# Cross-attention unit: both outer key products together, the sixth projection with the next unit's first, the middle key product behind them

## The reference, cut to what matters

```
q_hk  = (hidden_q @ Wq.T).reshape(B, S, H, K)
q_big = rope(einsum('bshk,hkq->bshq', q_hk, w_kc_q))      # 192 wide per head
q_r   = einsum('bshq,hqr->bhsr', q_big, W_qr)
k_r   = einsum('bld,hdr->bhlr', rope(kv_c), W_kr)
attn  = softmax(einsum('bhsr,bhlr->bhsl', q_r, k_r))
ctx_c = einsum('bhsl,bld->bhsd', attn, rope(kv_c))
out   = (einsum('bhsd,hkd->bhsk', ctx_c, w_kc_kv) -> B, S, H*K) @ Wo.T
```

## Time and profile before

| what | value |
|---|---|
| median of 3 runs | 451.5 us (450.04 to 451.88) |
| profiled execution, its own time | 454.02 us |
| span of that execution in the trace | 452.2 us |
| mean granted TensorE clock | 0.943 of full speed |
| attention units in the span | 211.3 to about 367.6 us |
| busy over the span | PE 82%, DVE 74%, ACT 47%, POOL 31% |

### The profile page before, as it was taken

One profiled execution on the slowest core, in us unless ns is written; L12 is line 12 of the kernel. 1 busy time (PEld: TensorE's weight loads), 2 busy tenths in 40 slices (PEclk: granted clock), 3 DMA queues, 4 the chain that ended last, 5 costly groups with the idle time before them and its releaser, 6 DMA issues.

```text
span 452.2 us, 10550 instructions
## 1 busy us (share of the span) xinstructions
PE 373.0 (82%) x3676; PEld 257.6 (57%) x3677; DVE 335.7 (74%) x836; ACT 213.0 (47%) x467; POOL 139.3 (31%) x149
## 2 busy tenths in 40 slices
PE   2497888833777778997999999999999989729995
PEld 1376666731344445774466475575664778516784
DVE  6849999888889889579776886887777525672453
ACT  1689999461577788684021131132122221324441
POOL 1110000023477774311092440431421410143334
PEclk9999999855699999999999999999999999957999
DMA  8995680402146551271022022021120201333011
GB/s 259 404 407 196 235 321 5 188 1 64 37 157 223 181 161 48 77 250 40 0 94 94 1 95 92 4 94 43 53 94 10 87 1 48 140 95 92 25 37 37
DMA packets 17183, 50.77 MB, mean 112 GB/s; under 512 B 2104, under 2 KB 6464, under 8 KB 15088
## 3 DMA queue, kind: packets, MB, share of 16 engines
q1 hardware_dynamic: 14272, 42.46, 26.3%
q0 software_dynamic: 2864, 7.68, 5.9%
HBM read 43.44 MB, written 6.69 MB: 111 GB/s over the span
## 4 chain that ended last, share of the span: by engine, by line
PE 56%; ACT 11%; DVE 10%; issue 8%; DMA 7%; POOL 5%; SPq 2%; DVEq 0%; ACTq 0%; POOLq 0%
PE bank L960 16%; PE bank L1174 8%; PE bank L976 6%; PE bank L1048 5%; DMA raw<-in_L_ffn_w_dram 3%; ACT W L1207 3%; PE bank L987 3%; PE bank L1001 2%; POOL y_rows L591 2%; PE bank L819 2%; PE bank L1027 2%; PE bank L1011 2%; ACT pnat L1193 2%; PE bank L830 1%; POOL xg L584 1%
## 5 line engine op out<-in xcount | busy, mean ns | idle before, releaser
L1714 DVE TENSOR_TENSOR roped<-bank,cst 128x512 f32<-128x512 f32 x96 | 61.1, 684 | 29.0 <-PE bank L960 28.0
L612 POOL TENSOR_TENSOR WE<-WE,wT 128x512 f32<-128x512 f32 x32 | 42.6, 1359 | 81.6 <-DMA WE<-_L_ffn_expert_masks_dram 81.6
L960 PE MATMUL bank<-XNT_hi,AW_hi 128*128 128x512 f32 x96 | 41.8, 435 | 0.5 <-DVE XNT_lo L1766 0.5
L1343 ACT ACTIVATE qrT<-bank 128x512 f32<-128x512 f32 x16 | 8.7, 596 | 62.2 <-PE bank L987 62.2
L960 PE MATMUL bank<-XNT_lo,AW_hi 128*128 128x512 f32 x96 | 37.8, 393 | 0.0
L960 PE MATMUL bank<-XNT_hi,AW_lo 128*128 128x512 f32 x96 | 37.5, 391 | 0.0
L976 PE MATMUL bank<-roped,MW 128*64 128x512 f32 x128 | 31.0, 605 | 0.0
L1337 ACT ACTIVATE prob<-prob 128x512 f32<-128x512 f32 x16 | 10.1, 632 | 44.3 <-DVE prob L1724 44.3
L1048 PE MATMUL bank<-VW,ctxT 128*128 128x256 f32 x128 | 30.7, 385 | 0.0
L584 POOL DMA_INDIRECT xg<-x_rows,owner_b x23 | 22.7, 985 | 23.5 <-DMA x_rows<-xrow 14.3
L960 PEld LDWEIGHTS bank<-XNT_hi,AW_hi 128*128 128x128 f32 x96 | 18.0, 187 | 19.9 <-issue 11.4
(11 more groups left out here) (305 smaller groups left out, 880.2 us busy)
## 6 DMA issues: line engine op xcount, KB each, us to landing
raw<-in_L_ffn_w_dram SPq DMA_DIRECT2D x8, 1536.0 KB, 8.9
fold<-in_L_xattn_fold_dram SPq DMA_DIRECT2D x8, 1024.0 KB, 5.0
WE<-_L_ffn_expert_masks_dram SPq DMA_DIRECT2D x8, 1024.0 KB, 5.3
kv<-in_keys_values_dram SPq DMA_DIRECT2D x8, 656.0 KB, 7.7
yg<-y_rows SPq DMA_DIRECT2D x8, 256.0 KB, 4.8
x_tok<-pay SPq DMA_DIRECT2D x8, 256.0 KB, 2.2
X<-in_x_dram SPq DMA_DIRECT2D x4, 256.0 KB, 11.8
x_rows<-xrow SPq DMA_DIRECT2D x1, 516.0 KB, 4.9
```

The lines of the kernel that those rows point to most:

```text
L612: pool.tensor_tensor(WE[:, e], WE[:, e], wT[:], ALU.mult).then_inc(WE_ready, 1)
L960: mm = pe.matmul(bank[g][:], a[:, k, c * P:(c + 1) * P], b[:, k, g * 512:(g + 1) * 512], start=k == 0 and i == 0, stop=k == 1 and i == 2)
L1714: ins = dve.tensor_tensor(roped[n][:, r, :].rearrange("p (b s) -> p b s", s=S), src, cst[:, None, at:at + S].to_broadcast([P, 8, S]), ALU. ...
```

## The change

Within each unit TensorE's blocks are written in another order: O1 moves ahead of P5, and P0' moves ahead of M.

```diff
                 project(u, 3)
                 project(u, 4)
                 to_keys_outer(u, 0)
+                to_keys_outer(u, 1)
                 project(u, 5)
-                to_keys_outer(u, 1)
-                to_keys_middle(u)
                 if u + 1 < NU:
                     project(u + 1, 0)
+                to_keys_middle(u)
                 if u:
                     turn_probs(u - 1)
```

## The result

The changed kernel takes 457.63 us (median of 5 runs, 456.88 to 463.63) against 450.77 for the kernel before (5 runs, 448.98 to 451.88): a ratio of 1.0175, 95% interval 1.0132 to 1.0218, which is 6.0 to 9.8 us. It is slower, as forecast, by 6.9 us and not by 10.0, and the median lies 1.2 us under the range that was given. The profiled execution is the slowest of the five, 463.63 us, with a span of 461.8.

A forecast was written before the change was run, and what follows sets the result against it. TensorE was taken as the bound, so new idle time is paid in full: 8.0 us (units 1 to 6), 1.87 (unit 7) and 0.06 (unit 0) make 9.97, taking 451.5 to 461.5 us; range 458.8 to 463.2, at 91%.

The forecast's parts named there:

- The chain of waits: Units 1 to 7: later P5 delays rope 5, then by_sum, so T waits about 1.2 us; unit 7's M waits 1.5.
- P5 "1.87 later": In each unit P5 follows O1 and so starts 1.87 us later, at 274.41 against 272.54 in unit 3's times.
- the head of P0': P0' directly behind P5 loses its first matmul's head: a gain of at most 0.11 us a unit, 0.8 in all.
- "A stalled T": T that waits for by_sum takes 0.14 us more itself, from 0 to 0.2, in each of units 1 to 6.
- waited with the matmul: Unit 7 before the change: T's weight load and matmul both start at 349.43, taken against loads running ahead across a wait.
- Behind the stretch, nothing: Everything from P1' on moves by one amount, VectorE's part too, so no later stall is saved or added.
- Unit 0: Unit 0 has no T; M starts some 0.05 us late and P1' about 0.06 later, counted as 0.06.
- the unit's term of 1.34 us: Units 1 to 6 each grow by 1.20 us of waiting plus 0.14 for T, bounds 1.20 to 1.40; 8.0 in all.
- 1 us either way for the scatter of medians: Allowance added to the sum's bounds because the three runs differ by 1.8 us, giving 459.5 to 463.0.
- T did not find its probabilities ready: Rival: by_sum ends by 279.25, T follows M at once, each unit gains 0.11 us, 450.7 us in all; 3%.
- 0.35 us was given back and not half: Rival: attention delays meet something later that did not move, half is hidden, 456.5 us; 4%.
- the clock did not fall in the units: Rival: gaps of 1.24 us lower the clock for a third of units 1 to 7, 42 us more, 503; 2%.

## Why the prediction was right or wrong

**The chain of waits was right**, though not the price at T. P5 1.72 us later, rope 5 with it, by_sum behind rope 5, T waiting for by_sum in units 1 to 7, M for rope 5 in unit 7 alone (1.5 us, as said), no later stall and no clock lost in the units: each is in the trace at its place. The experiments show it from three sides: O1 alone makes the whole delay (19.10 a unit), M alone next to none (17.85), and taking half of by_sum out from behind rope 5 takes T's wait away under the same order on TensorE (17.66).

**The sum was too large**, 9.97 us against 8.45 in the stretch and 8.1 with what lies behind it. Two of its terms were mis-sized and one was put at nothing:
- *P5 "1.87 later".* I took O0 and O1 as two blocks of 1.87; run together they take 276.40 − 272.81 = 3.59, so P5 comes 1.72 later. The 1.87 holds the change from one kind of matmul to another (about 0.15), which two blocks of a kind don't pay between them. I had priced only the head of P0', and in the sum of a unit T's wait swallowed that gain. Over units 1 to 6 this is 0.9 us, and in unit 7 it is the difference of 1.73 to 1.87.
- *"A stalled T", 0.14 a unit.* The wait costs T nothing beyond itself. In the changed kernel it takes 283.40 − 282.56 = 0.84 with its wait, and with only M moved 0.85 without one; in unit 7 it takes 0.93 with the wait and, with the sums split there, 0.93 without. What sets its time is its neighbours: 0.79 between two projections, 0.85 from M to a projection, 0.93 from M to `project_out`. So the step was a wrong reading of the earlier trace rows, and its true size is the 0.05 that T loses by standing behind M: 0.5 us less over six units. The load that "waited with the matmul" starts with it behind M whether T waits or not, so these rows don't show that a wait held the load back, as the prediction read them.
- *Behind the stretch, nothing.* There 0.3 to 0.4 us came back: from unit 7's scores to L1111 14.29 and 14.25 us against 14.60 and 14.65. I had held that the waits there move with the rest. One of them shrank: T of the last probabilities waits 0.44 us and not 0.75, because VectorE's multiply ahead of it overlaps less with POOL's mask multiply. The scores of unit 7 come 6.64 us behind the start of M and came 6.32 behind it, and the mask load hangs on M. Before, and then changed:

```profile
354.15 4.96 POOL L612 TENSOR_TENSOR WE<-WE,wT 128x512 f32<-128x512 f32 x4 [12.84 <-DMA WE<-_L_ffn_expert_masks_dram]
358.35 1.30 DVE L1730 TENSOR_TENSOR prob<-prob,s_stat 128x512 f32<-128x512 f32 x1
```

```profile
362.15 4.97 POOL L612 TENSOR_TENSOR WE<-WE,wT 128x512 f32<-128x512 f32 x4 [13.63 <-DMA WE<-_L_ffn_expert_masks_dram]
366.68 0.99 DVE L1730 TENSOR_TENSOR prob<-prob,s_stat 128x512 f32<-128x512 f32 x1
```

The multiply is 0.31 us shorter, and so is the whole piece; in the second traces both differ by 0.4.

Unit 0 cost 0.03 instead of 0.06. Together the unit's term of 1.34 us was 1.11.

**The range failed at its lower end.** The traces' own difference, 8.45 − 0.35 = 8.1 us, gives 1.018, inside both measured intervals. From the 451.5 of three runs it gives 459.6, inside the range, and from the 450.77 of the second set of runs 458.9, at its edge. So the mis-sized terms (1.9 us) and the base (0.7) used up the range, and "1 us either way for the scatter of medians" did not hold the 1.2 us that remain. Where those 1.2 us are isn't shown; the interval of the measured ratio, 6.0 to 9.8 us, holds 8.1 as well as 6.9. What the record shows is that pieces of executions come and go: 1.7 us with the low clock behind the units, and 4.1 us (before) and 4.6 us (changed) in when the attention begins. The mean granted clock of each run hints that the mix differs. Of 53 timed runs of the kernel before with a listed clock 17 have 0.942 or more, with a median of 450.22, and the others 451.69; of the 11 timed runs of the changed kernel 10 do, with 457.58. But like for like that is still 7.4 and not 8.1 us, and the mean clock doesn't tell which stretch was low: the trace with only M moved has 0.939 and no low clock behind the units.

The rivals: T did not find its probabilities ready; 0.35 us was given back and not half; the clock did not fall in the units. That the clock can fall behind an idle time inside the units came up only in the experiments (0.51 after 3.13 us, with both sums first).

**What is open.** Where the last 1.2 us between the traces and the medians are, and some 2 us of the gain of the split sums. Also why TensorE has idle times called issue: 3.13 and 2.86 us with both sums first, 0.84 with only M moved, 0.55 with one sum first, none in the attention of the unedited kernels. That a late packet and the load in its way make 2.2 of the 3.1 us fits the two traces; the remaining 0.9 us, with no load in flight, was not settled.

## What to carry to other kernels

Moving a block on the bound engine moves its product's reader too, and everything that stands behind that reader in the other engine's fixed order: ask what the next wait needs from the end of that queue, not only from the tile that was moved. When such a chain appears, look at the idle time of the waited-for engine first; half of by_sum put into 3.2 us of waiting (with the old order in the last unit) gave back all 8 us. A price read where a block waits (here 0.93 for T) is a price of the wait only if the same block between the same neighbours is cheaper without it. And a range for a difference of medians needs a term for pieces that come and go in whole executions, beside the terms of the sum.

## What the runs showed of the hardware

- TensorE stood still for 3.13 us amid one group of matmuls with no wait shown, while a 1 MB load filled the DMA engines (a share of 0.66 over the 3.9 us before) and a 16 KB packet on the instruction queue came at 262.5 us; with the load moved the packet came at 260.5 and the idle time was 0.94 us. That the packet held it is not shown.
- Its granted clock was 0.51 for 3.2 us after that one idle time, and fell to 0.50 after others of 2.86 and 1.77 us and after a wait of 2.37 us at M; it stayed at 1.00 after one of 1.70 us, through eight of 1.47 us (only O1 moved) and through seven of 1.08 us, 18.8 us apart.
- A wait of 1.08 us ahead of T cost just the wait: the eight transposes behind M took 0.84 us with it and 0.85 without, and their weight load started with the matmul either way.
- A VectorE multiply with both inputs in SBUF went from 0.69 us to 1.19 in the mean and 1.79 in the row shown beside a POOL multiply, and from 0.69 to 1.30 in the kernel before at its last probabilities; one whose large input is in PSUM (rope) kept 0.68. The Trainium skill (SBUF — State Buffer, the section on two separate sides) says that a VectorE operation with two SBUF inputs and a GpSimd operation that reads SBUF share a port pair that one holds for a whole instruction. The trace agrees that the two contend (POOL's four multiplies took 5.45 us there and 4.96 in the kernel before); it doesn't show for how long one holds the ports.
- A change between O's kind of matmul and a projection's cost about 0.15 us at full clock: 3.59 us for two outer blocks in a row against 2 × 1.87.
